# Left tap of the convolution scaled by ScalarE and added by GpSimd, rounding by GpSimd, three convolution buffers

## The reference, cut to what matters

```python
def act_quant(x):
    scale = 127.0 / jnp.clip(jnp.max(jnp.abs(x), axis=-1, keepdims=True), 1e-05)
    return jnp.clip(jnp.round(x * scale), -128, 127) / scale
...
h = bit_linear(x, w1)                                    # 256 -> 1024
h = depthwise_conv1d(h.transpose(0, 2, 1), conv_w, conv_b)
h = h.transpose(0, 2, 1)
h = jax.nn.silu(h)
return bit_linear(h, w2)                                 # 1024 -> 256
```

## Time and profile before

| what | value |
|---|---|
| median of 3 runs | 740.35 us (739.17 to 745.89) |
| the profiled execution | 735.44 us, span in the trace 733.4 us |
| VectorE busy over the span | 392.4 us (53%) |
| ScalarE busy over the span | 359.8 us (49%) |
| GpSimd busy over the span | 131.3 us (18%) |
| the stage of the change | from 644.5 us to the end, 88.9 us |

### The profile page before, as it was taken

The page is one execution under the profiler, slowest core; times in us unless marked ns, Lnnn a source line. Parts: engine busy times, 40 slices in busy tenths (PEclk is TensorE's granted clock), DMA queues, the critical chain, the costliest instruction groups (busy, mean ns, idle before and its releaser), DMA issues. The chain is left out here.

```text
span 733.4 us, 14478 instructions
## 1 busy us (share of the span) xinstructions
PE 561.1 (77%) x5309; PEld 478.7 (65%) x5309; DVE 392.4 (53%) x1176; ACT 359.8 (49%) x832; POOL 131.3 (18%) x189
## 2 busy tenths in 40 slices
PE   4799999998358008999999972469999999717743
PEld 3677887877237008999998962468788888515642
DVE  3667666666321701243323244457767677568775
ACT  2788778876120003323232312268888888645420
POOL 1132433341200260000000017202222222100000
PEclk9999999999756557999999995589999999958778
DMA  6211111110298256545454402401111110000001
GB/s 162 98 46 64 66 65 45 44 44 1 61 359 265 76 196 209 197 162 197 163 195 165 145 29 81 163 1 44 42 45 43 43 45 4 2 1 0 1 0 50
DMA packets 38200, 66.33 MB, mean 90 GB/s; under 512 B 4626, under 2 KB 29299, under 8 KB 38004
## 3 DMA queue, kind: packets, MB, share of 16 engines
q1 hardware_dynamic: 35444, 55.59, 23.1%
q0 software_dynamic: 2688, 9.83, 4.2%
HBM read 51.00 MB, written 14.42 MB: 89 GB/s over the span
## 5 line engine op out<-in xcount | busy, mean ns | idle before, releaser
L824 PE MATMUL a_ring<-ident,a_e 112*125 112x112 f32 x768 | 101.6, 283 | 4.2 <-ACT a_e L445 4.0
L824 PEld LDWEIGHTS a_ring<-ident,a_e 112*125 112x125 f32 x768 | 90.1, 191 | 21.4 <-issue 13.1
L1155 ACT ACTIVATE ex_h_t<-ex_h,b_e 128x128 f32<-128x128 f32 x168 | 47.9, 368 | 96.9 <-PE ex_h L1407 96.9
L453 ACT ACTIVATE a_et<-a_ring 125x448 f32<-125x448 f32 x128 | 62.8, 542 | 48.3 <-PE a_ring L824 48.3
L610 DVE CUSTOM_DVE_ANT_0 a_e<-a_s,a_mask 112x375 f32<-112x375 f32 x128 | 65.3, 543 | 31.5 <-issue 18.2
L1407 PE MATMUL ex_h<-ex_xg_t,w_s 128*128 128x128 f32 x672 | 80.9, 280 | 0.1
L1407 PEld LDWEIGHTS ex_h<-ex_xg_t,w_s 128*128 128x128 f32 x672 | 79.1, 197 | 0.5 <-DVE ex_xg_t L1302 0.5
L603 DVE TENSOR_REDUCE a_mx<-a_s 112x2 f32<-112x750 f32 x64 | 59.7, 933 | 35.7 <-PE a_s L815 35.7
L1419 PE MATMUL ex_y<-w_s,ex_h_t 128*128 128x256 f32 x336 | 75.8, 379 | 0.0
L445 ACT ACTIVATE a_e<-a_e,a_shift 112x375 f32<-112x375 f32 x128 | 69.1, 599 | 3.9 <-DVE a_shift L615 2.8
L1419 PEld LDWEIGHTS ex_y<-w_s,ex_h_t 128*128 128x128 f32 x336 | 62.3, 190 | 7.6
(11 more groups left out here) (254 smaller groups left out, 815.2 us busy)
## 6 DMA issues: line engine op xcount, KB each, us to landing
w_s<-in_L_ffn_W SPq DMA_DIRECT2D x21, 1024.0 KB, 5.0
w_all<-in_L_ffn_W SPq DMA_DIRECT2D x8, 1024.0 KB, 12.0
ct_dram<-a_ct SPq DMA_DIRECT2D x8, 752.0 KB, 4.4
a_ct<-ct_dram POOLq DMA_DIRECT2D x8, 752.0 KB
a_ctx<-in_ctx SPq DMA_DIRECT2D x8, 375.0 KB
x_slots<-ex_zeros SPq DMA_DIRECT2D x1, 2688.0 KB
ex_xg<-x_slots SPq DMA_DIRECT2D x21, 128.0 KB, 4.8
y_slots<-ex_y_sb SPq DMA_DIRECT2D x21, 128.0 KB, 1.7
```

The costliest lines, as they stand in the source:

```text
L453: a.activation(et[:, t % 2, kc], bank("et", t, kc)[0:KP, 0:4 * S], ACT.Copy)\
L824: last = nc.tensor.transpose(bank("et", t, kc)[0:KP, r * S:(r + 1) * S], es[:, t % 2, r, kc * KP:(kc + 1) * KP], ident[0:S, 0:S])
L1155: last = a.activation(h_t[:, i % 2, f], hb[i % 2][:, f * 128:(f + 1) * 128], ACT.Gelu, bias=b1_e[:, i % 2, f:f + 1])
```

## The change

- The left tap leaves VectorE. ScalarE scales the product by w0 into a new buffer `left[:, n % 2]` right behind `middle` (counter `c_scaled`), and GpSimd adds that buffer to `conv` (counter `c_left`). The right tap stays on VectorE and waits for GpSimd's addition.
- `conv` has three buffers in place of two. `middle(n)` now waits for `silu` of n - 3, and ScalarE takes `middle(j + 2)` before `silu(j)`, one step further ahead than before.
- The rounding proper moves from VectorE to GpSimd; VectorE keeps the multiplication, which now waits until GpSimd has released the `hr` buffer of n - 2.
- TensorE's list is not edited, and neither are the maxima, the scales or the second product.

```diff
-                conv = sb("bf_conv", [128, 2, HB, S])
+                conv = sb("bf_conv", [128, 3, HB, S])
+                left = sb("bf_left", [128, 2, HB, S - 1])
...
+                    @block.gpsimd
+                    def _(pool):
+                        g = nc.gpsimd
+
+                        def left_tap(half, j):
+                            n = FC * half + j
+                            pool.wait_ge(c_scaled, n + 1)
+                            g.tensor_tensor(conv[:, n % 3, :, 1:S], conv[:, n % 3, :, 1:S], left[:, n % 2], ALU.add).then_inc(c_left, 1)
+
+                        def rounded(half, j):
+                            n = FC * half + j
+                            pool.wait_ge(hr_out, n + 1)
+                            g.tensor_scalar(hq[:, j, columns(half)], hr[:, n % 2], NR, NR, ALU.add, ALU.subtract).then_inc(hq_out, 1)
+
+                        for j in range(FC):
+                            left_tap(0, j)
+                        for j in range(FC):
+                            left_tap(1, j)
+                            if j >= 5:
+                                rounded(0, j - 5)
+                        for j in range(3, FC):
+                            rounded(0, j)
+                        for j in range(FC):
+                            rounded(1, j)
...
                         def middle(half, j):
                             n = FC * half + j
                             act.wait_ge(u_ps, n + 1)
+                            if n >= 3:
+                                act.wait_ge(s_out, n - 2)
+                            a.activation(conv[:, n % 3].rearrange("p b s -> p (b s)"), pu[n % 3][:, 0:HALF], ACT.Identity,
+                                         bias=cb[:, j:j + 1], scale=cw[:, j, 1:2]).then_inc(c_mid, 1)
                             if n >= 2:
-                                act.wait_ge(s_out, n - 1)
-                            a.activation(conv[:, n % 2].rearrange("p b s -> p (b s)"), pu[n % 3][:, 0:HALF], ACT.Identity,
-                                         bias=cb[:, j:j + 1], scale=cw[:, j, 1:2]).then_inc(c_mid, 1)
+                                act.wait_ge(c_left, n - 1)
+                            a.activation(left[:, n % 2], pu[n % 3][:, 0:HALF].rearrange("p (b s) -> p b s", b=HB)[:, :, 0:S - 1],
+                                         ACT.Copy, scale=cw[:, j, 0:1]).then_inc(c_scaled, 1)
...
                         for half in range(2):
                             upper(half)
                             middle(half, 0)
+                            middle(half, 1)
                             for j in range(FC):
-                                if j + 1 < FC:
-                                    middle(half, j + 1)
+                                if j + 2 < FC:
+                                    middle(half, j + 2)
                                 silu(half, j)
...
                         def taps(half, j):
...
-                            dve.wait_ge(c_mid, n + 1)
-                            v.scalar_tensor_tensor(conv[:, n % 2, :, 1:S], u[:, :, 0:S - 1], cw[:, j, 0:1], conv[:, n % 2, :, 1:S],
-                                                   ALU.mult, ALU.add).then_inc(c_left, 1)
                             dve.wait_ge(c_left, n + 1)
...
                             dve.wait_ge(r_ps, half + 1)
+                            if n >= 2:
+                                dve.wait_ge(hq_out, n - 1)
                             v.tensor_tensor(hr[:, n % 2], hs[:, j, columns(half)], pr[:, 0:HALF], ALU.mult).then_inc(hr_out, 1)
-                            dve.wait_ge(hr_out, n + 1)
-                            v.tensor_scalar(hq[:, j, columns(half)], hr[:, n % 2], NR, NR, ALU.add, ALU.subtract).then_inc(hq_out, 1)
```

More of the change, by code:

```diff
@@ L1492, in bit_ffn_phase @@
                 c_mid = sem("bf_c_mid")
+                c_scaled = sem("bf_c_scaled")
                 c_left = sem("bf_c_left")
@@ L1553, in silu @@
                             act.wait_ge(c_right, n + 1)
-                            a.activation(hs[:, j, columns(half)], conv[:, n % 2].rearrange("p b s -> p (b s)"),
+                            a.activation(hs[:, j, columns(half)], conv[:, n % 3].rearrange("p b s -> p (b s)"),
                                          ACT.Silu).then_inc(s_out, 1)
@@ L1618, in taps @@
                             u = pu[n % 3][:, 0:HALF].rearrange("p (b s) -> p b s", b=HB)
-                            dve.wait_ge(c_mid, n + 1)
-                            v.scalar_tensor_tensor(conv[:, n % 2, :, 1:S], u[:, :, 0:S - 1], cw[:, j, 0:1], conv[:, n % 2, :, 1:S],
-                                                   ALU.mult, ALU.add).then_inc(c_left, 1)
                             dve.wait_ge(c_left, n + 1)
-                            v.scalar_tensor_tensor(conv[:, n % 2, :, 0:S - 1], u[:, :, 1:S], cw[:, j, 2:3],
-                                                   conv[:, n % 2, :, 0:S - 1], ALU.mult, ALU.add).then_inc(c_right, 1)
+                            v.scalar_tensor_tensor(conv[:, n % 3, :, 0:S - 1], u[:, :, 1:S], cw[:, j, 2:3],
+                                                   conv[:, n % 3, :, 0:S - 1], ALU.mult, ALU.add).then_inc(c_right, 1)
                         def highest(half, j):
```

## The result

| | before | changed |
|---|---|---|
| median | 740.68 us (4 runs) | 772.63 us (4 runs, 772.11 to 774.8) |
| ratio | | 1.0428, 95% interval 1.038 to 1.0475 |
| span of the profiled execution | 733.4 us | 770.5 us |

The change costs 32 us, 4.3%. The forecast was 765 with a range of 752 to 770: the direction and the loop were right, the range missed by 2.6 us, and one term, the rounding's price, had the wrong sign in its effect.

The account below looks back on a forecast made before the run. VectorE was taken to bound both halves before the change. Halves +15.2 and +12.3 us, tail -1.3 and -1.9, sum +24.3: from 735.44 to 759.7, or 765 us on the median's scale; range 752 to 770.

Parts of the forecast that it names:

- the loop: Both halves: middle(m+1) needs up(m+1), which stands behind highest(m-2), which needs silu(m-2), just ahead of middle(m+1); +15.2 and +12.3 us.
- the rounding's price: Rounding proper on GpSimd: 0.65 us each, upper end 1.14, taken from copies and two-input additions.
- VectorE's freed time brings nothing: Both halves: 17 us of busy time leave VectorE, but it no longer sets the pace, because of the order.
- The rival that it doesn't bind: Both halves: TensorE's product is ready when silu ends, ScalarE sets the pace at 2.19 us a chunk; 740 us, chance 0.05.
- The size of a turn: One chunk's round of waits between ScalarE and TensorE: 4.69 us at 1.2 GHz, 3.61 at 2.4, against 1.90 before.
- The gap between the halves at 0: Between the halves the same steps (copy, subtraction, product) wait for each other as before: 0 us change.
- The half clock: TensorE in the halves: too little work to keep the full clock or regain it; 4.69 us a turn instead of 3.61.
- The rival with a full clock in most turns: TensorE holds 2.4 GHz or regains it in most turns: +14.7 us, 755 us, chance 0.18.
- GpSimd's addition: Left tap added to conv on GpSimd: 1.14 us for 444 columns, costing nothing except in the ends of the halves.
- VectorE's wait for the `hr` buffer binds: Tail: would bind only if GpSimd is slower than 0.65 us; multiplications waiting for GpSimd would show the forecast wrong.
- The tail: TensorE's two waits for rounded chunks before the second products: 1.3 and 1.9 us shorter, with five and eight roundings left.
- the rival with dear rounding: GpSimd's rounding costs 1.14 us like its two-input addition; waits +1.4 and +2.4, sum +31.3: 771 us, chance 0.10.

Follow-up runs that it names:

- experiment one: The changed kernel with TensorE's transposes for the maxima and VectorE's maxima one chunk later: 758.4 us, ratio to before 1.0213.
- experiment seven: The kernel before with only three convolution buffers and ScalarE's middle one step further ahead, GpSimd doing nothing: 755.9 us, ratio 1.0174.
- experiment six: The changed kernel with four unread extra products ahead of TensorE's transposes, in the first half and chunks 2 to 5 of the second: 765.2 us, ratio 1.0292.
- Experiment two: The changed kernel with the rounding proper back on VectorE and without VectorE's wait for the released hr buffer: 764.3 us, ratio to before 1.0324.
- experiment four: The kernel before plus sixteen GpSimd operations on scratch tiles behind the last addition to x; ran once, only lengths used: the rounding's form 1.73 and 1.71 us.
- Experiments two and three: Experiment two, and the kernel before with only its rounding proper moved to GpSimd: the latter 750.4 us, ratio 1.0147.

## Why the prediction was right in its loop and wrong in its size

- **What bounds, and that VectorE's freed time brings nothing:** right. In experiment one a chunk takes 1.80 us on ScalarE where VectorE needed 1.90.
- **The loop between two lists:** right, shown three ways: the waits in the trace, its removal (18.9 us less in the stage, the clock's part included), and its appearance without any of GpSimd's work (experiment seven). The rival that it doesn't bind is out.
- **The size of a turn:** 4.40 and 3.27 us, not 4.69 and 3.61. I took 0.74 us between starts of activations from a pair of rows whose second had to wait for VectorE's right tap, which ended at 667.17 (666.49 + 0.68). Back to back they start 0.62 and 0.51 us apart, less than their lengths of 0.72 and 0.62. Three of the nine turns ran at the full clock besides. Over both halves and the gap the forecast was 27.5 us more, measured 23.3.
- **The gap between the halves at 0:** wrong by 0.8 us. The second half's transposes stand behind those for the maxima in TensorE's list and so behind the loop, at half the clock. With the loop but the full clock (experiment six) the gap is 3.9 us again, so the 0.8 us are the clock's.
- **The half clock:** right in the main, and in part by luck. Of the nine turns that hold nothing else, six ran at 0.50 and three at 1.00; experiment six gives 7.1 us for the half clock. The rival with a full clock in most turns is out for the changed kernel. But the reason that I gave, "too little work to keep the full one, too little to get it back", isn't shown. Experiment two kept 1.00 over three such turns. And the row from 679.0 to 685.7 that I read as 75% busy is a stretch without work up to 680.71 and unbroken work behind it (5.00 us busy of the 5.00 from 680.70 to 685.70, at 0.50): its average says nothing of a turn with work in half of it. The Trainium skill (TensorE: Matmul & The Clock Gate, What's actually happening), read to the letter, would have kept the full clock; the trace has TensorE idle never longer than 1.80 us at a time in these turns, and in six of nine the clock was down. What decides between them stays open.
- **GpSimd's addition:** 1.05 us, 1.14 forecast; hidden, as said, but for the ends of the halves.
- **GpSimd's rounding, the step that failed:** "it does two operations, so I take 0.65, with 1.14 as the upper end". Measured 1.71, half again above my upper end. That end was the price of two inputs; experiment four measures 1.12 us for two inputs and 1.71 to 1.73 for one input with two constants. So VectorE's wait for the `hr` buffer binds, which I had named as a sign of being wrong. GpSimd also had six roundings left after the last `silu`, where I had placed five, since one had stood behind the last left tap. The tail is 10.4 us longer where I had 3.2 shorter: 13.6 us of error. Experiments two and three show it, by taking the rounding away from GpSimd (10.4 us less in the waits) and by giving it nothing else (10.2 more). The trace of before had a GpSimd operation with a constant (257 ns for 4 columns), too narrow to give a slope, and I put the copies' slope under it; it also had a power of two inputs that took 1042 ns for 4 columns, a warning that the form can weigh more than the width. The Trainium skill (GPSIMD Engine Reference, Key points) has VectorE about 2x faster elementwise: measured 1.05 to 0.67 for the added tap, 1.6, and 1.71 to 0.394 for the rounding, 4.3.
- **The sum:** the miss in the stage is 10.4 us (34.7 measured, 24.3 forecast): 13.6 from the rounding, 1.0 from the second products, less 4.2 from turns that I had too long. In the medians 7.6 us of it show. That the time came out only 2.6 us above the range is luck, two errors against each other; so is that the rival with dear rounding summed to 771. It named the mechanism, but with 1.14 us a rounding it had 3.8 us in the waits where 10.4 were measured, and the long turns made up for most of the rest.
- **Order in GpSimd's list:** not looked at. A rounding ahead of the last left tap delays the last `silu` of the second half by 1.4 us.

## What to carry to other kernels

Before an engine is made to run further ahead, write the lists of two engines side by side and look for the step at which each one's next instruction needs the other's last: a deeper buffer doesn't open a wait that comes from list order, and the half clock that TensorE met in most of these turns is a second bill (1.13 of 4.40 us). When work moves to another engine, take the price from that engine's own rows of the same kind of operation and nearly the same width; if there are none, the upper end is open, and the most nearly related row isn't a bound.

## What the runs showed of the hardware that I had not expected

On GpSimd, with no other engine computing, a 128 x 448 f32 tile costs 0.56 us to copy, 1.12 to add to another, 1.33 to add to a constant, and 1.72 to add and subtract constants, to f32 or bf16 alike. Behind a `middle` of 0.72 us, which reads PSUM, ScalarE starts its next activation 0.62 us after the start, so a sum of lengths overstates a run of them. Work added to a waiting TensorE made the changed kernel's stage 7.1 us shorter through the clock alone.
